# Four conv blocks on one core: the second image's front data loaded whole, its statistics and tokens placed earlier, the outputs of the first image two steps later

## The reference, cut to what matters

```python
def _gn(v, G=32, eps=1e-5): ...        # mean and variance of 12 channels x 48 x 48 pixels
# layer 0: a Mamba block over the 2304 pixels of an image (a scan)
# layer 1:
t = jnp.einsum('bchw,oc->bohw', x, w_in)          # 384 -> 384 channels
tf = jnp.fft.rfft2(t in 8x8 patches) * fft_filter; t = irfft2(tf)
t = conv3x3 depthwise(t, w_dw)                     # 384 channels
x1, x2 = t[:, :192], t[:, 192:]
y = jnp.einsum('bchw,oc->bohw', gelu(x1) * x2, w_out)
# layer 2: depthwise 11x11 convolution whose kernels are 4 weighted points
out = lax.conv_general_dilated(x, kernels[:, None], padding=5, groups=384)
# layer 3: a mixture of 4 experts with top-2 gates, per pixel
```

## Time and profile before

| | |
|---|---|
| median of 3 runs | 5398.89 us (5396.8 to 5402.14) |
| the profiled execution, its own time | 5385.23 us |
| its span, from the first to the last instruction | 5383.1 us |
| PE busy | 4668.1 us (87%) |
| DVE busy | 4369.6 us (81%) |
| ACT busy | 3078.8 us (57%) |
| POOL busy | 2963.6 us (55%) |
| mean granted TensorE clock | 0.965 |

### The profile page before, as it was taken

How to read it: one execution, slowest core, us unless ns; L and a number is a source line. 1 busy time by engine, 2 the same in 40 slices (tenths; PEclk the granted TensorE clock), 3 DMA queues, 4 the chain that set the end, 5 groups by cost and what they waited for, 6 DMA issues and landing times. The chain is left out here.

```text
span 5383.1 us, 78300 instructions
## 1 busy us (share of the span) xinstructions
PE 4668.1 (87%) x28407; PEld 3758.7 (70%) x28407; DVE 4369.6 (81%) x4973; ACT 3078.8 (57%) x6415; POOL 2963.6 (55%) x3552
## 2 busy tenths in 40 slices
PE   4888888888888888888888887779898888999999
PEld 2666666666666666666666665447676777999999
DVE  1999999999999999999999997667677764656555
ACT  3777777777777777777777774323233232333333
POOL 3776777777777776777777764455545420000000
PEclk8999999999999999999999998879898999999999
DMA  2001000001000001000000001210201021121110
GB/s 77 1 13 33 10 10 10 10 13 33 10 10 10 10 14 32 10 10 10 10 10 10 10 5 43 84 44 26 85 20 40 26 71 53 45 59 55 49 59 29
DMA packets 101597, 155.71 MB, mean 29 GB/s; under 512 B 5804, under 2 KB 98268, under 8 KB 101212
## 3 DMA queue, kind: packets, MB, share of 16 engines
q1 hardware_dynamic: 101212, 150.71, 8.8%
HBM read 108.07 MB, written 42.61 MB: 28 GB/s over the span
## 5 line engine op out<-in xcount | busy, mean ns | idle before, releaser
L744 DVE TENSOR_TENSOR_SCAN a_h<-a_dA,pw 128x771 f32<-128x771 f32 x1152 | 2014.4, 1751 | 116.5 <-PE pw L451 115.6
L600 ACT ACTIVATE a_dA<-a_dt,a_Aneg 128x384 f32<-128x384 f32 x2304 | 1345.4, 607 | 152.1 <-DVE a_h L744 147.2
L462 PEld LDWEIGHTS pw<-g_ident,a_h 128*128 128x128 f32 x6912 | 783.6, 142 | 618.4 <-DVE a_acc L763 268.3
L882 POOL TENSOR_SCALAR a_dBT<-a_dtxT,a_BC 128x768 f32<-128x768 f32 x1152 | 1025.0, 907 | 298.6 <-PE pw L451 213.9
L462 PE MATMUL pw<-g_ident,a_h 128*128 128x128 f32 x6912 | 980.6, 279 | 227.7 <-DVE a_acc L763 158.0
L451 PE MATMUL pw<-g_ident,a_dBT 128*128 128x128 f32 x6912 | 953.9, 275 | 4.8 <-POOL a_dBT L882 4.8
L763 DVE SCALAR_TENSOR_TENSOR a_acc<-pw,a_BC,a_acc 128x768 f32<-128x768 f32 x912 | 914.2, 1002 | 51.1 <-PE pw L462 46.8
L451 PEld LDWEIGHTS pw<-g_ident,a_dBT 128*128 128x128 f32 x6912 | 802.2, 142 | 6.5 <-POOL a_dBT L882 5.4
L834 POOL TENSOR_TENSOR a_xin<-a_xin,a_tm 128x384 f32<-128x384 f32 x432 | 433.0, 1002 | 34.4 <-ACT a_tm L521 9.0
L1875 DVE TENSOR_TENSOR d_hf<-d_hf,d_wb 128x384 f32<-128x384 f32 x288 | 159.2, 558 | 310.0 <-ACT d_hf L1814 300.6
L894 POOL TENSOR_TENSOR a_acc<-a_acc,a_tm 128x768 f32<-128x768 f32 x168 | 307.2, 1829 | 161.2 <-ACT a_tm L614 160.2
(11 more groups left out here) (230 smaller groups left out, 9096.3 us busy)
## 6 DMA issues: line engine op xcount, KB each, us to landing
b_xs<-x SPq DMA_DIRECT2D x36, 576.0 KB, 4.0
d_wb<-cw SPq DMA_DIRECT2D x24, 768.0 KB, 5.8
a_xs<-in_x SPq DMA_DIRECT2D x24, 576.0 KB, 3.9
x<-a_xs SPq DMA_DIRECT2D x24, 576.0 KB, 3.0
b_x<-x SPq DMA_DIRECT2D x24, 576.0 KB, 4.4
e_xs<-x SPq DMA_DIRECT2D x24, 576.0 KB, 3.8
out<-e_xs SPq DMA_DIRECT2D x24, 576.0 KB, 5.8
a_sx<-in_x SPq DMA_DIRECT2D x54, 192.0 KB, 2.3
```

The costliest lines, as they stand in the source:

```text
L462: t = e.transpose(m["pw2"][:, c * 128:(c + 1) * 128], m[f"a_h{g % 2}"][:, c // 2, first_col(c) + tb * 128:first_col(c) + (tb + 1) * 128], ...
L600: e.activation(dA[:, first_col(c):first_col(c) + T], m[f"a_dt{k % 2}"][:, c, :], ACT.Exp, scale=m["a_Aneg"][:, c, n:n + 1]).then_inc(s["a_ ...
L744: e.tensor_tensor_scan(m[f"a_h{g % 2}"][:, p % 3, :], m[f"a_dA{pi % NDA}"][:], m[f"pw{pi % 2}"][:, COL:COL + PAIR], 1.0, ALU.mult, ALU.add ...
L882: t = e.tensor_scalar(m[f"a_dBT{g % 2}"][:, tb, :], m[f"a_dtxT{o}"][:, tb, :], m[f"a_BC{o}"][:, tb, n:n + 1], 1.0, ALU.mult, ALU.mult)
```

## The change

Five things are altered. (1) The tables move from `b_x1`'s place to that of `b_cv1` and the buffers behind it; `b_cv1`'s first use waits for `v_m`. (2) Image 1 is loaded whole into `b_x1` right behind the tables' loads and ahead of `store0`; its twelve strip loads and their wait go, and `strip` reads image 1 from `b_x1`. (3) Image 1's statistics are due from step 8 instead of 24 and its norm at 22 instead of 29.2. (4) Image 0's outputs are due 2.2, 2.2 and 1.2 steps later, image 1's tokens 0.2 earlier; the gates hang on the outputs' due times. The head is due at 58.2 instead of 57.2, its patches closer together, and image 2's statistics at 60 instead of 55. (5) The third channel tile (ACT and POOL) of image 1's first convolution group leaves the front and is due in steps 0.3 to 3.9 of image 0's units; group 1's is due at 4.2 instead of 1.5. Some due times within a token step move by some tenths (`read_at`). No instruction of an engine's arithmetic is added or taken away.

```diff
@@ -231,11 +231,11 @@
     m.new("b_ti", [128, 3, 50, 50])
-    for i in range(2):
-        m.new(f"b_cv{i}", [128, 3, 2 * T])
+    m.new("b_cv0", [128, 3, 2 * T])
+    mats = m.at
+    m.new("b_cv1", [128, 3, 2 * T])
     for i in range(2):
         m.new(f"b_tm{i}", [128, 2 * T])
-    mats = m.at
     m.new("b_x1", [128, 3, L])
@@ -977,7 +977,7 @@
     if b == 1:
-        return 31 + 1.9 * min(n, 11) + 0.9 * max(0, n - 11)
+        return 30.8 + 1.9 * min(n, 11) + 0.9 * max(0, n - 11)
     return 4 + 2.4 * n
@@ -986,13 +986,27 @@
     if g == 0:
-        return (52.5 if b == 1 else 44.5) + k
+        return 52.5 + 0.9 * k if b == 1 else 44.5 + k
     return 1.5 + 11.5 * (g - 1) + 1.15 * k
 def out_at(b, g, i):
-    at, gap = (((31, 0.9), (42.2, 0.9), (53.4, 0.5)) if b == 0 else ((7.8, 0.6), (14.2, 0.9), (25.8, 0.8)))[g]
+    at, gap = (((33.2, 0.9), (44.4, 0.9), (54.6, 0.5)) if b == 0 else ((7.8, 0.6), (14.2, 0.9), (25.8, 0.8)))[g]
     return at + gap * i
+
+
+def third_at(b, g, k):
+
+    if b == 1 and g == 0:
+        return 0.3 + 0.45 * k
+    if b == 1 and g == 1:
+        return 4.2 + 0.75 * k
+    return conv_at(b, g, k)
+
+
+def read_at(b, n, i):
+
+    return ((0.5, 0.6, 0.6) if b == 0 else (0.5, 0.7, 0.8) if b == 1 and n > 10 else (1.0, 1.3, 1.5) if b == 1 else (0.8, 1, 1.1))[i]
@@ -1197,7 +1211,7 @@
     march([early(post_pe(e, m, w, S, D, NCH - 1), POST), norm_pe(e, m, w, O, 0, 2.6), tokens_pe(e, m, w, 0), outputs_pe(e, m, w, O, 0),
-           norm_pe(e, m, w, O, 1, 29.2), tokens_pe(e, m, w, 1), head_pe(e, m, w, O, 0, 57.2, 61)], 0)
+           norm_pe(e, m, w, O, 1, 22), tokens_pe(e, m, w, 1), head_pe(e, m, w, O, 0, 58.2, 61.8)], 0)
     for b in range(NB):
@@ -1218,13 +1232,13 @@
         if n < NT:
-            yield win_at(b, n) + 0.5
+            yield win_at(b, n) + read_at(b, n, 0)
             u = NT * b + n
         if n >= 2:
-            yield win_at(b, n) + 0.6
+            yield win_at(b, n) + read_at(b, n, 2)
             u = NT * b + n - 2
@@ -1238,13 +1252,15 @@
     for k in range(9):
-        yield conv_at(b, g, k)
+        yield third_at(b, g, k)
         dy, dx = divmod(k, 3)
             w.wait_ge("pe_wo", 6 * (3 * b + g - 1))
+            if b == 0 and g == 1:
+                w.wait_ge("v_m", 4)
             e.activation(dst, src, ACT.Copy, scale=dw[:, 2, 0:1]).then_inc(s["a_c2"], 1)
@@ -1317,7 +1333,7 @@
     march([early(post_act(e, m, w, NCH - 1), POST), tokens_act(e, m, w, 0), matrices_act(e, m, w), conv_act(e, m, w, 0, 0), conv_act(e, m, w, 0, 1),
-           conv_act(e, m, w, 0, 2), gelu_act(e, m, w, 0), tokens_act(e, m, w, 1), conv_act(e, m, w, 1, 0), head_act(e, m, w, 0, 61)], 0)
+           conv_act(e, m, w, 0, 2), gelu_act(e, m, w, 0), tokens_act(e, m, w, 1), head_act(e, m, w, 0, 61.8)], 0)
     for b in range(NB):
@@ -1325,6 +1341,8 @@
         if b + 1 < NB:
+            if b == 0:
+                side.append(conv_act(e, m, w, 1, 0))
             side += [conv_act(e, m, w, b + 1, 1), conv_act(e, m, w, b + 1, 2), gelu_act(e, m, w, b + 1), head_act(e, m, w, b + 1, 51.5)]
@@ -1333,9 +1351,9 @@
-    if b == 0:
-        return m["b_x0"][:, :, rows(r)], f"d_x0{r}", 16
-    j = 2 * NQ * (b - 1) + NQ * again + r
+    if b < 2:
+        return m[f"b_x{b}"][:, :, rows(r)], f"d_x{b}{r}", 16
+    j = 2 * NQ * (b - 2) + NQ * again + r
     return m[f"b_xs{j % 3}"][:], f"d_t{j % 3}", 16 * (j // 3 + 1)
@@ -1367,7 +1385,7 @@
     for n in range(NT):
-        yield win_at(b, n + 1) + 0.6
+        yield win_at(b, n + 1) + read_at(b, n + 1, 1)
         u = NT * b + n
@@ -1516,8 +1536,8 @@
            conv_dve(e, m, w, 0, 0), conv_dve(e, m, w, 0, 1), conv_dve(e, m, w, 0, 2), gated_dve(e, m, w, 0), outputs_dve(e, m, w, 0),
-           pieces_dve(e, m, w, 1, 24, 0.7), norm_dve(e, m, w, 1, 29.2), tokens_dve(e, m, w, 1), conv_dve(e, m, w, 1, 0), head_dve(e, m, w, 0, 57.2, 61),
-           pieces_dve(e, m, w, 2, 55, 1)], 0)
+           pieces_dve(e, m, w, 1, 8, 0.9), norm_dve(e, m, w, 1, 22), tokens_dve(e, m, w, 1), conv_dve(e, m, w, 1, 0), head_dve(e, m, w, 0, 58.2, 61.8),
+           pieces_dve(e, m, w, 2, 60, 0.8)], 0)
     for b in range(NB):
@@ -1566,7 +1586,7 @@
     for k in range(1, 9):
-        yield conv_at(b, g, k) + 0.3
+        yield third_at(b, g, k) + 0.3
         pr = 24 * b + 8 * g + k - 1
@@ -1605,7 +1625,7 @@
         for c in range(CT):
-            yield at + 0.5 * c
+            yield at + (0.25 if b == 0 else 0.5) * c
             w.wait_ge("p_sw", 6 * (b + 1))
@@ -1626,8 +1646,7 @@
     march([early(post_pool(e, m, w, NCH - 1), POST), norm_pool(e, m, w, 0, 2.6), tokens_pool(e, m, w, 0), conv_pool(e, m, w, 0, 0), conv_pool(e, m, w, 0, 1),
-           conv_pool(e, m, w, 0, 2), gated_pool(e, m, w, 0), norm_pool(e, m, w, 1, 29.2), tokens_pool(e, m, w, 1), conv_pool(e, m, w, 1, 0),
-           head_pool(e, m, w, 0, 57.2, 58.5, 59, 60)], 0)
+           conv_pool(e, m, w, 0, 2), gated_pool(e, m, w, 0), norm_pool(e, m, w, 1, 22), tokens_pool(e, m, w, 1), head_pool(e, m, w, 0, 58.2, 59.6, 59.9, 60.7)], 0)
     for b in range(NB):
@@ -1635,6 +1654,8 @@
         if b + 1 < NB:
+            if b == 0:
+                side.append(conv_pool(e, m, w, 1, 0))
             side += [conv_pool(e, m, w, b + 1, 1), conv_pool(e, m, w, b + 1, 2), gated_pool(e, m, w, b + 1), head_pool(e, m, w, b + 1, 32.2, 38, 43, 50.6)]
@@ -1671,27 +1692,23 @@
         e.dma_start(m[f"b_{n}"][:], d[n]).then_inc(s["d_l2"], 16)
+    for r in range(NQ):
+        load(1, r)
     store0(e, m, d, w, NCH - 1)
-        j = 2 * NQ * (b - 1) + NQ * again + r
+        j = 2 * NQ * (b - 2) + NQ * again + r
         if r >= 3:
             w.wait_ge("v_b1", GN * b + 3 * (r + 4))
-        elif b > 1:
+        elif b > 2:
             w.wait_ge("p_na", 3 * (NQ * (b - 1) + r + 4))
-    for again in range(2):
-        for r in range(NQ):
-            passing(1, r, again)
-    w.wait_ge("v_m", 4)
-    for r in range(NQ):
-        load(1, r)
     for r in range(NQ):
```

## The result

| | before | after |
|---|---|---|
| median | 5396.87 us (5381.42 to 5402.14, 8 runs) | 5365.76 us (5348.97 to 5379.82, 8 runs) |
| ratio | | 0.9944, 95% interval 0.9926 to 0.9963 |
| profiled execution, its span | 5385.23, 5383.1 us | 5352.32, 5350.2 us |
| PE, DVE, ACT, POOL busy | 4668.1, 4369.6, 3078.8, 2963.6 us | 4645.3, 4376.8, 3082.0, 2968.5 us |
| mean granted clock | 0.965 | 0.970 |

The eight runs after the change lie in two groups, four from 5349 to 5357 us and four from 5375 to 5380, so the median is the middle of a gap in which no run lies; a place where two traces of the kernel part is shown in experiment 12. The same kernel timed once more gave a ratio of 0.9960, about 22 us, so "31 us" is no more exact than some ten microseconds.

The account below looks back on a forecast made before the run. In the front no engine is full; waits passing between in-order lists and DVE's work set the length. Terms 22.6 + 7.9 - 2 = 28.5 us gave 5356.7 us profiled, 5370.4 us timed; range 5353 to 5390.

Parts of the forecast that it names:

- The load costs nothing: Front: image 1, loaded whole at the tables' loads, is there by 3345 us, before its first DVE reader at about 3356.
- Statistics and norm: Front, image 1: moving both early takes 11.0 us of statistics and 6.6 us of norm waits off DVE's stretch.
- Gates: Front, second and third group: DVE's waits of 5.63 and 5.61 us ahead of its gates go; gain 11.2 us.
- new waits: Front: 6.1 us at image 0's first output (between 0 and 12) and about 3 us in the third group.
- the second wait: Front, third group: PE's tokens 11 and 12 wait for the gate, about 3 us, bounds 0 and 5.6.
- Sum to the head's matmul: Front: 11.0 + 6.6 + 11.2 + 2.9 - 6.1 - 3, the head's group matmul 22.6 us earlier.
- Image 2's statistics: Front: due at 60 instead of 55, they leave the path to the head; gain 2.9 us.
- The head: From group matmul to first sparse matmul: 21.1 us instead of 28.97, gain 7.9 us, or 3.7 with slow patches.
- The units: Image 0's units: the eight moved adds make PE wait longer for the token strip; loss 2 us, bounds 0 and 16.2.
- Waits coming back in the front: Front: gates give nothing and the first output's wait doubles; gain only 11.2 us, 5388 us; chance 0.22.
- POOL's backlog: Image 0's units: all 16.2 us of adds delay patches and strips; gain only 14.3 us, 5385 us; chance 0.07.
- The clock: Front: new waits hold PE at its lower clock level; kernel up to about 41 us slower, 5440 us; chance 0.04.

Follow-up runs that it names:

- experiment 12: The changed kernel run once more, unaltered; median 5374.4 us, ratio 0.9960 to the kernel before.
- experiment 1: The kernel before with only the change's load of image 1 and its buffers, all due times as before; median 5393.8 us, ratio 0.9995.
- experiment 6: The changed kernel with image 0's first output put ahead of image 1's first two token matmuls on PE; median 5374.1 us, ratio 0.9960 to the kernel before.
- strip first: The changed kernel with seven of the eight moved adds behind image 2's power and first strip on POOL; median 5377.3 us, ratio 0.9969 to the kernel before.
- experiment 7: The changed kernel with the third channel tile of image 1's first convolution group back in the front; median 5368.1 us, ratio 0.9948 to the kernel before.
- experiment 8: Same run as "strip first": the changed kernel with the moved adds due later on POOL; first store 53.3 us behind the first sparse matmul, ratio 0.9969.
- experiment 11: The changed kernel with that third tile in POOL's wait ahead of the head, group 1's due as before, DVE's taps closer; median 5357.6 us, ratio 0.9937.

## Why the prediction came out right, term by term

The median of 5365.8 us is inside the range and 4.6 us from the forecast of 5370.4. That closeness is in part luck: none of the eight runs lies between 5357 and 5374 us, and the same kernel's second ratio puts it at about 5377 us on the forecast's scale (5398.9 x 0.9960). The signs hold but for the last: image 0's units, up to the load that waits for their last store, took 260.2 us before, 256.9 in the first trace and 268.0 in the second, not 2 us more. The terms don't hold.

- **The load costs nothing:** right, by experiment 1.
- **Statistics and norm, 17.6 us together:** the step that failed. "11.0 us of DVE time leave the stretch" is true of DVE's time and false of the path. Without the data wait the term is 15.6 us; done alone it was worth 7.6 us, undone 3.4 to 9.8. In this stage, which no engine fills, part of what DVE saved came back as a wait: 4.5 us more at the first gate.
- **Gates, 11.2 us, less 6.1 and 3 us of new waits:** by these terms the outputs' shift would be worth 2.1 us. Undone it cost 12 to 19, waits and granted clock together. The gates' part was sized about right (15.3 us of waits for three gates, 5.4 of them at the first, which the term left out). The first output's wait came as foreseen, 8.00 us for 6.1, partly because both token matmuls ran at the lower clock (4.21 us, not 3.93 and 2.20). That it is to be charged is not borne out: experiment 6 took it away, and no gain is shown. Of the second wait, priced at 3 us, PE shows 1.79 us ahead of a token matmul behind the third gate.
- **Sum to the head's matmul, 22.6 us:** measured 20.2 and 18.4, and 24.7 by "strip first". Two errors with opposite signs cancelled, statistics and norm 6 to 12 us too high and the outputs' shift 10 to 16.5 us too low. That is luck. Image 2's statistics (2.9 us) were not tried by themselves.
- **The head, 7.9 us:** 9.5, of which the adds are 4.4 by experiment 7. The patches went at 0.644 us as assumed. Matmul and small rows until the power took 2.51 us, not 3.26 (the matmul 1.62 for 2.38), and DVE's tap pair ahead of the last scale 1.94 us, not 2.67, with POOL still: together 1.5 of the 1.6 us by which the chain beat the term.
- **The units, -2 us:** -5.6 us up to the first store. The token matmul came 21.4 us behind, as worked out, but the wrong instruction was followed: in experiments 7 and 8 it stands at 15.4 us both times, with the store at 42.2 and 53.3 us. Where the adds stand, not the strip, sets this store; in POOL's gap they cost 6 to 6.5 us less.
- **Rivals.** Waits coming back in the front: the gates' waits stayed away and the first output's was 8.00 us, not the doubled 12.2, and it isn't shown to cost anything. (Of POOL's 71.4 us there, 70.6 were for `b_tm`.) POOL's backlog: there, at a third of its price. The clock: in the front it rose, 0.92 for 0.83, with the waits at the gates gone; the threat was real in another place, behind the front, where one and the same kernel is 4.7 us shorter or 11.1 us longer than the kernel before, with 1.00 or 0.66 granted where its two traces part. By the Trainium skill (TensorE: Matmul & The Clock Gate, "HAM oscillation — how this bites in real kernels") bursts with idle waits between lower the clock; the rows agree and don't suffice: the drop of the repeat follows a wait of PE for image 0's patches of 2.35 us, and the first trace has the same wait, 2.64 us, and no drop.

## What to carry to other kernels

Where no engine is full, don't add up an engine's busy time: walk the path. Work taken off it can come back as a wait at the next instruction that depends on another engine (here 4.5 us did), and a wait seen there may be worth little. Change the order so that each in-order list has ready work ahead of the wait; up to the head that gave more here than taking work away did. Before work is moved, look for the idle stretch that is already there (33 us of POOL ahead of the head) rather than the next stage. And for a gain under 1% take the same kernel's trace twice before reading a difference between two kernels.

## What the runs showed of the hardware

A tap, a DVE instruction with two SBUF inputs, depends on what POOL does. In the changed kernel, taps alone by shape, from 3431 to 3517 us with POOL's adds beside them and from 3517.6 to 3558 us with POOL nearly still:

```profile
L1412 DVE SCALAR_TENSOR_TENSOR b_cv<-b_ti,b_dw,b_cv 128x768 f32<-128x768 f32 x33 | 49.7, 1548 | 0.1
```

```profile
L1412 DVE SCALAR_TENSOR_TENSOR b_cv<-b_ti,b_dw,b_cv 128x768 f32<-128x768 f32 x16 | 15.5, 1011 | 0.0
```

1548 and 1011 ns, and up to 2.56 us in experiment 11; the adds beside them average 2.2 us there for 1.80. The clearest case is one small POOL instruction at the changed kernel's head, which takes 0.26 to 0.27 us elsewhere in that chain and took 1.82 us beside a pair of taps, ending 0.06 us behind it (DVE, then POOL):

```profile
3555.72 1.94 DVE L1412 SCALAR_TENSOR_TENSOR b_cv<-b_ti,b_dw,b_cv 128x768 f32<-128x768 f32 x2
```

```profile
3555.90 1.82 POOL L1624 TENSOR_SCALAR b_sw<-b_wn,b_sc 128x4 f32<-128x4 f32 x1 [1.55 <-DVE b_sc L1474]
3557.70 0.27 POOL L1625 TENSOR_SCALAR b_bw<-b_wn,b_sc 128x4 f32<-128x4 f32 x1
```

The Trainium skill (SBUF — State Buffer, "SBUF: two separate sides") has it that the two engines exclude each other on one port pair; the rows agree in kind. The prediction used one mean, 1335 ns, for both situations.

The other is the granted clock of the stage behind: two lengths, 1780 and 1796 us, of one program, whose two traces differ by 0.1 us at the first store and by 4.3 us at the second.
